# Moving the max-abs pass over the second FFN weight from one block ahead of the attention loop into its four chunks

## The reference

```python
x = x + _layernorm(attn(_layernorm(x)))
x = x + _layernorm(ffn(_layernorm(x)))
# attn: qk = silu(x @ Wqk.T); v = silu(x @ Wv.T); four heads with rope
#   lin_kv = einsum('bgnd,bgne->bde', lk, v) / n
#   out = silu(x @ Wg.T) * (relu(quad_att)**2 @ v + lq @ lin_kv);  out @ Wo.T, layernorm
def fake_quant_weight(w):
    scale = jnp.max(jnp.abs(w)) / 127
    return jnp.clip(jnp.round(w / scale), -128, 127) * scale
# ffn: h = gelu(x @ quant(W_fc).T + LoRA);  h @ quant(W_proj).T + LoRA
```

## Time and profile before

| | us |
|---|---|
| median of 3 runs | 2304.24 |
| lowest, highest | 2299.45, 2341.54 |
| the profiled execution | 2305.27 |
| its span on the slowest core (core 3) | 2303.7 |
| spans of all 8 cores | 2268.0 to 2303.7 |
| busy on core 3: PE, DVE, ACT, POOL | 1223.0, 768.5, 325.7, 153.7 |

### The profile page before, as it was taken

One profiled execution on the slowest core, in us unless ns is written; L12 is line 12 of the kernel. 1 busy time (PEld: TensorE's weight loads), 2 busy tenths in 40 slices (PEclk: granted clock), 3 DMA queues, 4 the chain that ended last, 5 costly groups with the idle time before them and its releaser, 6 DMA issues.

```text
span 2303.7 us, 17295 instructions; the slowest of 8 cores (2268.0 to 2303.7 us)
## 1 busy us (share of the span) xinstructions
PE 1223.0 (53%) x5596; PEld 525.8 (23%) x5596; DVE 768.5 (33%) x1246; ACT 325.7 (14%) x437; POOL 153.7 (7%) x240
## 2 busy tenths in 40 slices
PE   1101389850564365266256405887554715998564
PEld 0000156520221122022122102332111302333221
DVE  3333332043221311411320157997983052000202
ACT  0012212210110210211110011221001011220001
POOL 1000000000111111011111100110110000000000
PEclk9999999975778689588778857999777957999887
DMA  1111285135353354244435433553442321222333
GB/s 20 28 55 46 83 197 123 19 114 160 30 57 64 50 50 70 46 46 64 64 37 59 69 52 100 162 164 133 164 160 96 112 80 37 61 67 74 106 109 105
DMA packets 178384, 191.89 MB, mean 83 GB/s; under 512 B 83717, under 2 KB 124678, under 8 KB 178231
## 3 DMA queue, kind: packets, MB, share of 16 engines
q1 hardware_dynamic: 79000, 130.68, 18.7%
q0 software_dynamic: 99296, 60.12, 17.9%
HBM read 204.70 MB, written 29.36 MB: 102 GB/s over the span
## 4 chain that ended last, share of the span: by engine, by line
PE 32%; DVE 24%; DMA 24%; issue 12%; ACT 6%; DVEq 1%; SPq 0%; POOL 0%; ACTq 0%; POOLq 0%
PE PC L235 10%; PE PBIG L235 10%; DMA AW<-wgT 6%; DMA WSLB<-scr_pj 6%; DMA WSLB<-woT 5%; PE PA L235 5%; PE PD L235 4%; DVE FSCR L523 3%; DVE FSC L527 3%; DMA XT<-wpjT 3%; ACT AZQ L244 3%; DVE ST L366 2%; DVE ST L364 2%; DVE ISCR L520 2%; DMA XT<-x 2%
## 5 line engine op out<-in xcount | busy, mean ns | idle before, releaser
L235 PE MATMUL PBIG<-WSLB,AV 128*128 128x512 bf16 x512 | 144.5, 408 | 170.7 <-DMA WSLB<-scr_pj 104.9
L364 DVE BATCH_NORM_STATS2 ST<-PBIG 128x6 f32<-128x512 f32 x16 | 11.1, 696 | 605.9 <-PE PBIG L232 605.9
L235 PE MATMUL PBIG<-IDENT,AZQ 128*128 128x128 bf16 x192 | 30.6, 296 | 304.4 <-DVE AZQ L909 132.0
L235 PE MATMUL PC<-AY,AW 128*128 128x512 bf16 x252 | 102.1, 574 | 136.8 <-DMA AW<-wgT 108.5
L235 PE MATMUL PBIG<-AY,AW 128*128 128x512 bf16 x704 | 159.1, 379 | 18.7 <-DVE AW L530 15.2
L743 DVE TENSOR_TENSOR AGT<-PA,GATEE 128x512 bf16<-128x512 f32 x64 | 44.3, 692 | 296.9 <-ACT GATEE L244 179.5
L235 PE MATMUL PBIG<-WSLB,AGT 128*128 128x512 bf16 x256 | 74.1, 416 | 96.7 <-DMA WSLB<-woT 92.2
L485 DVE TENSOR_REDUCE MXP<-XT 128x1 f32<-128x1024 f32 x64 | 77.9, 1220 | 131.7 <-DMA XT<-wfcT 77.5
L235 PEld LDWEIGHTS PBIG<-WSLB,AV 128*128 128x128 bf16 x512 | 44.1, 100 | 266.8 <-issue 237.2
L235 PE MATMUL PC<-QQ,QKK 128*128 128x128 bf16 x32 | 4.1, 307 | 189.6 <-ACT AZQ L244 112.3
L244 ACT ACT_TABLE_LOAD x15 | 19.2, 1283 | 540.1 <-DVE SA L1086 232.3
(11 more groups left out here) (230 smaller groups left out, 1893.6 us busy)
## 6 DMA issues: line engine op xcount, KB each, us to landing
XT<-wfcT SPq DMA_DIRECT2D x64, 512.0 KB, 4.5
XT<-wpjT SPq DMA_DIRECT2D x64, 512.0 KB, 4.1
WSLB<-scr_pj SPq DMA_DIRECT2D x96, 256.0 KB, 2.6
AW<-wgT POOLq DMA_DIRECT2D x64, 256.0 KB, 4.6
WSLB<-woT POOLq DMA_DIRECT2D x64, 256.0 KB, 4.3
XT<-x SPq DMA_DIRECT2D x16, 512.0 KB, 3.3
LKT<-scr_x SPq DMA_DIRECT2D x32, 256.0 KB, 3.2
scr_fc<-AW POOLq DMA_DIRECT2D x32, 256.0 KB, 2.3
```

The costliest lines, as they stand in the source:

```text
L235: e.matmul(o, a, b, start=s1, stop=s2))
L364: s1 = vop(lambda e: e.bn_stats(out=ST6[:, 0:6], in_=src[:, 0:512]), deps=deps)
```

## The change

`quant_max` is split in three: a function that only makes the state (no instruction), `quant_max_loads(st, rng)` with the loads and reductions of a range, and `quant_max_fin(st)` with the closing part. For W_fc all of it is still emitted where it was. For W_proj nothing is emitted ahead of `lin_kv` any more; chunk C of the attention loop emits loads and reductions 8C to 8C+7, after the next chunk's ropes and before the output projection, and chunk 3 the closing part too. Counts, sizes and buffers are as before.

```diff
-    def quant_max(w_hbm, cols, qsl, start_deps):
-        npc = (D * FF) // (128 * 1024)
-        for i in range(npc):
+    def quant_max_loads(st, rng):
+        for i in rng:
             b = i % 2
             stg = XT[:, b * 1024:(b + 1) * 1024]
             c, j = divmod(i, ncw2)
             ldt = dma("sync", stg, w2[:, c, j, :],
...
             xtp[b] = mx
+            st["mx_toks"].append(mx)
+
+    def quant_max_fin(st):
...
+    def quant_max(w_hbm, cols, qsl, start_deps):
+        st = dict(qsl=qsl, stores=[], mx_toks=[],
+                  w2=w_hbm.rearrange("(c p) (j k) -> p c j k", p=128, k=1024),
+                  ncw2=cols // 1024, start_deps=start_deps)
+        return st
...
     q_fc = quant_max(wfcT, FF, QS, last(y_done, tables_done, ld_b64))
+    quant_max_loads(q_fc, range(32))
+    quant_max_fin(q_fc)
...
             heads_nxt = (hq2, hk2, hl2)
+        quant_max_loads(q_pj, range(C * 8, (C + 1) * 8))
+        if C == 3:
+            quant_max_fin(q_pj)
```

More of the change, by code:

```diff
@@ L471, in build_nc @@
     xtp = [last(prev_z, tables_done), last(prev_z, tables_done)]
-    def quant_max(w_hbm, cols, qsl, start_deps):
-        npc = (D * FF) // (128 * 1024)
-        w2 = w_hbm.rearrange("(c p) (j k) -> p c j k", p=128, k=1024)
-        ncw2 = cols // 1024
-        mx_toks = []
-        for i in range(npc):
+    def quant_max_loads(st, rng):
+        w2 = st["w2"]
+        ncw2 = st["ncw2"]
+        for i in rng:
             b = i % 2
@@ L482, in quant_max @@
             ldt = dma("sync", stg, w2[:, c, j, :],
-                      deps=last(xtp[b]) + (list(start_deps) if i == 0 else []),
+                      deps=last(xtp[b]) +
+                      (list(st["start_deps"]) if i == 0 else []),
                       ctr_name="qld")
@@ L488, in quant_max @@
             xtp[b] = mx
-            mx_toks.append(mx)
+            st["mx_toks"].append(mx)
+    def quant_max_fin(st):
+        qsl = st["qsl"]
+        npc = len(st["mx_toks"])
+        mx_toks = st["mx_toks"]
         m1 = vop(lambda e, q=qsl, n=npc: e.tensor_reduce(
@@ L514, in quant_max @@
             deps=[sinv])
-        return dict(sinv=sinv, s=s_, s2=s2, sinv2=sinv2, qsl=qsl, stores=[])
+        st.update(sinv=sinv, s=s_, s2=s2, sinv2=sinv2)
+    def quant_max(w_hbm, cols, qsl, start_deps):
[3 more added lines that the diff above has]
+        return st
     def jit_quant(st, b, w_src, wf, wf_deps, stt_dst, store=True):
```

## The result

| | before | changed |
|---|---|---|
| median of 10 runs, us | 2299.52 | 2264.94 |
| lowest, highest | 2293.99, 2341.54 | 2255.92, 2282.91 |
| ratio, with its 95% interval | | 0.9846 [0.9813, 0.9878] |
| profiled execution: its time, span on the slowest core | 2305.27, 2303.7 (core 3) | 2268.58, 2267.0 (core 1) |
| spans of the 8 cores, mean | 2284.1 | 2251.8 |

The account below looks back on a forecast made before the run. PE's 77.35 us hole behind lin_kv, set by 30 W_proj loads, and output projections bound by DMA were taken as the limits. 2305.3 - 68.2 + 20.4 = 2257.5 us, rounded 2258 (-2.05%); range 2238 to 2282.

Parts of the forecast that it names:

- The removal: Between lin_kv and chunk 0's scores: without W_proj's block there, PE's hole shrinks from 77.35 to about 9.2 us; -68.2 us.
- The cover on DVE: In each chunk, eight reductions take 20.6 us, hidden under PE's output projection with 26 to 27 us of slack; cost 0.
- The contention: In the four output projections: W_proj's loads make Wo's loads 2.8 us late, 5.1 us lost per chunk; +20.4 us.
- that sign: In the output projections: Wo's loads land at about 7 us beside W_proj's loads, at a median of 4.2 outside.
- the upper bound of the prediction: In the output projections: all added DMA work pushes Wo's loads, 9.6 us per chunk, 38.6 us in four.
- The even turn: DMA engines alternate queues by packet, at most doubling a Wo load's moving part: 2.2 us late, some 17 us in all.
- The clock: In the output projections: longer waits may put more matmul groups at 1.2 GHz; 0 in the sum, 0 to 14 us in range.
- one of its signs of being wrong: In the output projections: a share of PE's granted clock clearly under 0.88 would show the forecast wrong.
- A: In the output projections: W_proj's loads fall into DMA gaps, at most 2.6 us lost per chunk; 2237 to 2247; chance 0.2.
- B: In the output projections: full contention, 38.6 us and up to 14 for the clock; 2270 to 2290 us; chance 0.22.
- C: Output projections starved of Wo's loads, slower than before; break-even 17 us per chunk; chance 0.02 over 2% slower, 0.03 below that.
- D: Behind lin_kv: something else holds PE until about 580, so the wait stays; 2305 to 2325 us; chance 0.03.

Follow-up runs that it names:

- a second look: The unchanged kernel before, profiled once more; its hole behind lin_kv was 72.0 us in the mean, 64.4 to 78.7 from core to core.
- the two filled kernels: Kernel before with six extra zero-adding matmuls behind each output-projection group, of one row or full array: 2300.93 and 2272.43 us, one run each.
- The time without any contention: Changed kernel without W_proj's 32 max-pass loads, reductions kept on stale data: 2249.06 us, ratio 0.9756.
- Half the bytes: Changed kernel with each W_proj load and reduction cut to 512 columns, 256 KB instead of 512 KB: 2256.70 us, one run; projections 235.9 us.
- the filled pair: Changed kernel and kernel before, each with six full-array zero matmuls behind each output-projection group: 2244.62 and 2272.43 us, one run each.

## Why the prediction was right, and what was off

*The removal: right in place and mechanism, too large by 3 to 12 us.* The hole shrank to the 9.2 us worked out, on every core and in every run without the block. The 68.2 us were those of one core in one execution, and on core 3 they came true (77.3 to 9.2, 68.1). But the hole before the change is set by how long 30 loads take, and that differs: 72.3 to 78.2 us over the cores of the same execution (mean 74.6, so 65.4 gained), 72.0 in a second look, 67.7 and 63.6 in the two filled kernels that keep the block. The time without any contention showed 56 us. The step that failed is the choice of one core's value for the term, where the hole on the other cores could have been read too.

*The cover on DVE: right.* 25 and 28 us of slack against 26 and 27 in the prediction. That the eight reductions would take 20.6 us was wrong (21.6 to 27.1), which the cover absorbed.

*The contention: right in its path and its sign, and near in size partly by luck.* 20.4 us were forecast, 26.7 came: late Wo loads do lengthen the stage, as worked out. But the term was built on them landing 2.8 us later, at about 7 us, and that sign did not come. On core 1 in chunk 0 they landed at a median of 5.2 us in the stretch with W_proj's loads and 4.5 behind it; over all cores the medians are 5.17 and 4.42:

```profile
DMA to landing us min/median/max: 4.0/5.2/7.6
...
DMA to landing us min/median/max: 4.0/4.5/4.8
```

That is 0.75 us between the medians, and 1.1 in the mean against the kernel before (5.4 and 4.3). The V projection's loads were a poor measure, as one consists of 1040 packets, nearly all of 512 B, against 144 for a Wo load, most of 2 KB (counted in the trace). The f32 loads, taken as undisturbed from the earlier trace rows, are slowed as well, to 6.0 us in this stage (5.4 in all stages of all cores):

```profile
WSLB<-woT POOLq DMA_DIRECT2D x14, 256.0 KB, 4.5
XT<-wpjT SPq DMA_DIRECT2D x6, 512.0 KB, 6.0
```

So the stretch, from the issue of a chunk's third load to the landing of its last, is 21.1 us in the mean and not 18.2. With 1.1 us of lateness in it the prediction's own working gives 21.1 x 1.1 / 8.3 = 2.8 us per chunk, 11 in all. That 20.4 stood nearer to the 26.7 is two errors against each other: a lateness over twice too large, and nothing for the clock and for waits that fall unevenly.

What holds in all runs as a measure is the upper bound of the prediction, with a factor: the DMA work that the loads add to the stage, 0.53 x 18.2 = 9.6 us by the prediction, 9.3 in the mean of the changed kernel's stages (counted from the packets), comes back as 6.7 us of length with two buffers (0.7 of it) and as 8.3 with four (0.9). Half the bytes gave half. The even turn of the Trainium skill (DMA: Bandwidth & Descriptors, Queues, rings and completion order) would have allowed a Wo load to be later by up to its own moving part, 2.2 us by the prediction's estimate; a median of 0.75 is no contradiction, and no run here shows the turns themselves. The 17 us worked out from it were too few by 10.

*The clock: 0 in the sum, up to 14 in the range.* The slow matmuls more than doubled, which the prediction had as a possibility only, and one of its signs of being wrong came true: the granted clock of these stages on core 1 is 0.79 to 0.86, under the 0.88 named. What it costs lies between nothing (the filled pair: 27.3 us apart with the clock held, 26.4 without) and 9.0 us (the estimate with the recorded loads), and zero in the sum had no row behind it: that the hole is shorter says nothing of the waits in the projections.

*The rivals.* A (contention nearly free, under 2.6 us per chunk) is excluded by 5.9 to 8.0 us in each of the four stages. B (full stacking) names both things that grew, DMA work and slow matmuls, but its 38.6 us and the clock's price on top were too much, and its sign, Wo's loads at 9 us and over, did not come (5.2). The time fell between the forecast and B. C and D did not occur: no stage lost 17 us, and nothing else held PE.

*Sum.* Removal 68.2 forecast against 65.4 in the mean of cores, contention 20.4 against 26.7, other stages 0 against +6 that no run could tie to the change: -47.8 against -32.3 in the mean of the cores, and -34.6 in the medians.

How the stage turns this lateness into 6.7 us can be followed most of the way. Only 23 of 64 Wo loads of a core met W_proj's, but means count here and not medians: the 14 loads issued within a stage take 4.81 us in the mean against 4.31 before, 6.9 us more in sum, and with two buffers in turn about half of that, 3.5 us, lies on the chain. The estimate above gives 4.4 for the later loads, uneven as they are (4.0 to 7.6 us on core 1), and 2.3 for the slower clock, together the 6.6 us by which a stage grew from its first to its last matmul. What stays open is the clock's part, why Wo's loads land sooner beside fillers, and what the loads wait for.

## What to carry to other kernels

Work that is moved out of a hole is not free because the engine that does it is idle at the new place: ask what its loads share with the transfer that the new stage waits for, and price them by the DMA engines' time (here 0.7 to 0.9 us of stage for each us added). The best place is a stage that waits for no transfer at all; here it was there from the start, under the V projection with a DMA share of 0.17. And where a stage waits for one load per tile with two buffers, more buffers are worth more than any placement: 27 us were at stake in the placing, but 92 in Wo's buffers (220.7 to 128.7) and some 148 in the gate part's (364.8 to 217.2).

## What the runs showed of the hardware

Two kinds of fillers left PE's clock in different places. With six matmuls of 1 x 512 behind each group of the changed kernel, core 5 ran from 1039.5 to 1060.9 us without a wait and at a granted clock of 0.52, nearly all at 1.2 GHz; with six of 128 x 512 in the same places the slow matmuls fell from 119 to 17 in the changed kernel and from 50 to 2 in the kernel before. And a count of slow matmuls is no price: 14.5 us by the count of 69, 9.0 by the estimate with the recorded loads, nothing by the filled pair. The fillers themselves changed what they were to leave alone, the loads' time to landing (4.2 to 3.5 us in the kernel before).
